# Attention of a two-layer kernel: four scores in a row, then the row maxima in groups of one and three

## The reference

```python
x = x + attn(layernorm(x))
# attn
Q = einsum('btd,hkd->bthk', x, W_Q) + b_Q        # K, V alike
scores = einsum('bqhk,bshk->bhqs', Q, K) / sqrt(64)
out_h = einsum('bhqs,bshk->bqhk', softmax(scores), V)
return einsum('bqhk,hdk->bqd', out_h, W_O) + b_O
```

## Time and profile before

| | |
|---|---|
| median of 3 runs | 1372.09 us (1371.39 to 1373.73) |
| the profiled execution's own time | 1373.44 us |
| its span, first to last instruction | 1371.1 us |
| TensorE (PE) busy | 1187.1 us, 87% |
| VectorE (DVE) busy | 919.2 us, 67% |
| ScalarE (ACT) busy | 568.5 us, 41% |
| GpSimd (POOL) busy | 749.8 us, 55% |
| exponentials, ACT L842 | 256 of 1026 ns |
| row maxima, DVE L1131 | 256 of 1225 ns |
| sums of probabilities, POOL L1572 | 180 of 2370 ns |

### The profile page before, as it was taken

How to read it: one execution, slowest core, us unless ns; L and a number is a source line. 1 busy time by engine, 2 the same in 40 slices (tenths; PEclk the granted TensorE clock), 3 DMA queues, 4 the chain that set the end, 5 groups by cost and what they waited for, 6 DMA issues and landing times. The chain is left out here.

```text
span 1371.1 us, 19083 instructions
## 1 busy us (share of the span) xinstructions
PE 1187.1 (87%) x7491; PEld 671.4 (49%) x7491; DVE 919.2 (67%) x1318; ACT 568.5 (41%) x735; POOL 749.8 (55%) x379
## 2 busy tenths in 40 slices
PE   4799979999999998999999999567876777676898
PEld 2345535555555554555555558555432333233676
DVE  4766566566566567466756445246999899996687
ACT  1244434444444445343444435238643622233544
POOL 1277756776777676465797821532754455464200
PEclk9999999999999999999999989778988889799899
DMA  5000000000000000000001142453622333240000
GB/s 173 1 1 2 1 1 1 1 1 2 1 1 2 1 1 1 2 1 1 5 9 32 55 174 76 132 215 123 203 92 92 107 110 110 93 150 0 0 17 16
DMA packets 38057, 68.82 MB, mean 50 GB/s; under 512 B 5936, under 2 KB 24112, under 8 KB 37968
## 3 DMA queue, kind: packets, MB, share of 16 engines
q1 hardware_dynamic: 32624, 47.75, 10.8%
q0 software_dynamic: 5344, 19.86, 4.1%
HBM read 61.30 MB, written 6.16 MB: 49 GB/s over the span
## 5 line engine op out<-in xcount | busy, mean ns | idle before, releaser
L1572 POOL TENSOR_TENSOR psums<-psums,prob 128x1024 f32<-128x1024 f32 x180 | 426.7, 2370 | 128.1 <-ACT prob L842 106.1
L1131 DVE TENSOR_REDUCE mx<-psum 128x2 f32<-128x1024 f32 x256 | 312.5, 1225 | 174.2 <-PE psum L458 163.7
L842 ACT ACTIVATE prob<-psum 128x1024 f32<-128x1024 f32 x256 | 261.2, 1026 | 266.3 <-PE psum L445 253.6
L472 PE MATMUL psum<-prob,V 128*64 128x512 f32 x1024 | 248.5, 605 | 0.0
L1632 POOL TENSOR_TENSOR hc<-hs,cc 128x1024 f32<-128x1024 f32 x64 | 155.4, 2427 | 167.4 <-DVE hs L1396 167.1
L700 PE MATMUL psum<-hc,ident 128*128 128x512 f32 x256 | 149.5, 714 | 53.2 <-POOL hc L1632 51.6
L1396 DVE TENSOR_TENSOR_SCAN hs<-dA,psum 128x1024 f32<-128x1024 f32 x64 | 146.3, 2286 | 2.1
L1572 POOL TENSOR_TENSOR psums<-prob 128x1024 f32<-128x1024 f32 x30 | 71.7, 2390 | 135.2 <-ACT prob L842 135.1
L441 PE MATMUL psum<-q_hi,k_hi 64*128 64x512 f32 x512 | 123.7, 473 | 1.6 <-issue 0.9
L472 PEld LDWEIGHTS psum<-prob,V 128*64 128x64 f32 x1024 | 69.1, 138 | 109.3 <-issue 105.8
L458 PE MATMUL psum<-k_hi,q_hi 64*128 64x512 f32 x512 | 109.1, 429 | 0.0
(11 more groups left out here) (234 smaller groups left out, 1693.0 us busy)
## 6 DMA issues: line engine op xcount, KB each, us to landing
cc<-C_rows SPq DMA_DIRECT2D x64, 512.0 KB, 3.7
slots_in<-e_zero SPq DMA_DIRECT2D x2, 960.0 KB, 8.6
slots_out<-e_y SPq DMA_DIRECT2D x30, 64.0 KB
slot_rows_h<-slots_in SPq DMA_DIRECT2D x6, 256.0 KB
x<-in_x SPq DMA_DIRECT2D x2, 512.0 KB, 5.2
e_w<-in_e_w SPq DMA_DIRECT2D x1, 1024.0 KB
out_x<-x SPq DMA_DIRECT2D x4, 256.0 KB, 2.3
wk<-in_wk SPq DMA_DIRECT2D x1, 512.0 KB, 4.3
```

Of the source, the lines that this page charges most:

```text
L472: ins = pe.matmul(A.O[HALF[s], :], A.V[pair % 2][:, j, s * DH:(s + 1) * DH], A.prob[unit(pair, c, j) % NPB][:, s * CH:(s + 1) * CH], start ...
L842: act.activation(A.prob[n % NPB][:, :], slots.bank("score", pair, c, j).rearrange("p s n -> p (s n)"), ACT.Exp, scale=float(DH) ** -0.5).t ...
L1131: dve.tensor_reduce(K.A.mx[:, :, t, c], slots.bank("max", pair, t, c), AXX, ALU.max).then_inc(*slots.inc("max", pair, t, c))
L1572: pool.tensor_tensor(total[:, :], (K.A.prob[(n - 1) % NPB] if j == 1 else total)[:, :], K.A.prob[n % NPB][:, :], ALU.add).then_inc(*K.psum ...
```

## The change

The order of steps within a phase is written differently. Before, the four maxima of a phase stand behind the four scores, one each, and `out` behind the last of them, ahead of the projection. Now the four scores stand in a row, one maximum behind them, then the projection and the first `pv`, then the other maxima (three; four or five in pair 0), `cols` and `out`, and then the second `pv`. `row` moves from the middle of P2 to the front of P3. `proj` is split in two steps, `proj` for TensorE and ScalarE and `lo` for VectorE, and `lo` stands right behind `proj` everywhere. P0 to P3 of pair 15 stay as they are.

```diff
@@ phase
-    order = []
-    for i, j in enumerate(js):
-        order.append(("score", pair, c, j))
-        order += [("max", *m) for m in maxes[len(maxes) * i // 4:len(maxes) * (i + 1) // 4]]
+    maxes = [("max", *m) for m in maxes]
+    order = [("row", nxt)] if f == 3 and nxt < PAIRS else []
+    order += [("score", pair, c, j) for j in js] + maxes[:1]
+    maxes = maxes[1:]
+    if pair == LAST and f == 1:
+        order += [("out", last, 0), ("out", last, 1)]
     if f == 2 and nxt < PAIRS:
-        order.append(("cols", nxt))
+        maxes.append(("cols", nxt))
     if pair < LAST and f >= 2 and last >= 0:
-        order.append(("out", last, f - 2))
-    elif pair == LAST and f == 1:
-        order += [("out", last, 0), ("out", last, 1)]
+        maxes.append(("out", last, f - 2))
     first, second, third = [], [], []
...
-        first = [("proj", ahead, *CHUNKS[(f + 1) % 4])]
+        first = [(kind, ahead, *CHUNKS[(f + 1) % 4]) for kind in ("proj", "lo")]
...
-    if f == 2 and nxt < PAIRS:
-        second = [("row", nxt)]
...
-    order += first + pv[:2] + second + pv[2:3] + third + pv[3:]
+    order += first + pv[:1] + maxes + pv[1:2] + second + pv[2:3] + third + pv[3:]
@@ plan_all
-        elif kind in ("proj", "row", "values", "sum", "sumhalf", "gdir"):
+        elif kind in ("row", "values", "sum", "sumhalf", "gdir"):
             work.plan("dve", *step)
-            if kind == "proj":
-                K.hi.plan(*k)
+        elif kind == "proj":
+            work.plan("dve", *step, now=False)
+            K.hi.plan(*k)
```

More of the change, by code:

```diff
@@ L202, in attention_order @@
     order = [("lnvar", 0), ("lnroot", 0), ("lnrows", 0), ("lnturn", 0), ("lncopy", 0), ("bias", 0)]
-    order += [("proj", 0, *ch) for ch in CHUNKS]
+    order += [(kind, 0, *ch) for ch in CHUNKS for kind in ("proj", "lo")]
     side = [("values", 0, 0), ("values", 0, 1)] + [("proj", 1, *ch) for ch in CHUNKS] + [("proj", 2, *CHUNKS[0])]
@@ L208, in attention_order @@
             order.append(side.pop(0))
+            if order[-1][0] == "proj":
+                order.append(("lo", *order[-1][1:]))
     order += [("cols", 0), ("row", 0)]
@@ L330 @@
 CHUNKED = ("fc1", "xpj", "inp", "dtp")
-EMPTIES = {"xr_out": "xr", "turned": "turn", "outp_out": "outp", "choose": "logits", "fc2_out": "fc2", "e1_lg": "e1_gate",
+EMPTIES = {"lo": "proj", "xr_out": "xr", "turned": "turn", "outp_out": "outp", "choose": "logits", "fc2_out": "fc2", "e1_lg": "e1_gate",
            "gelu": "up", "yrow": "down", "gelu1": "up1", "sum1": "sum1", "added": "turn1"}
@@ L1501, in dve_added @@
     ins.then_inc(*K.work.inc("turn1", b, c))
-DVE_STEPS = {"lnvar": dve_moments, "lnhalf": dve_half_moments, "lnrows": dve_rows, "bias": dve_bias, "proj": dve_proj, "max": dve_max, "pv": dve_late_sums, "cols": dve_cols,
+DVE_STEPS = {"lnvar": dve_moments, "lnhalf": dve_half_moments, "lnrows": dve_rows, "bias": dve_bias, "lo": dve_proj, "max": dve_max, "pv": dve_late_sums, "cols": dve_cols,
              "row": dve_row, "values": dve_values, "sum": dve_sum, "sumhalf": dve_sum_half, "out": dve_out, "gdir": dve_gdir, "choose": dve_choose,
```

## The result

| | before | after |
|---|---|---|
| median of 4 runs each, same chip | 1372.91 us (1371.39 to 1374.08) | 1390.29 us (1388.09 to 1392.08) |
| ratio | | 1.0126, 95% interval 1.0106 to 1.0147 |
| the profiled execution, and its span | 1373.44, 1371.1 | 1388.09, 1386.8 |
| ordinary pair (P0, P1, P2, P3) | 47.05 (11.82, 11.93, 12.18, 11.12) | 48.1 (11.5, 12.7, 12.1, 11.8) |

The account below looks back on a forecast made before the run. TensorE's own order of work was taken as the bound. Ordinary pairs +0.77 us, times 13 +10.0; special places +2.5 + 1.9 + 2.4 - 1.9 - 0.3 - 0.1; sum +14.5, giving 1386.6 us, range 1376 to 1397.

Parts of the forecast that it names:

- P0: First of a pair's four TensorE phases: nothing waits for VectorE, -0.38 us, to 11.44.
- P1: Second phase: the second values wait 1.1 us for VectorE, busy with the maxima; +0.72, to 12.65.
- P2 with the row: Third phase: output projection waits for VectorE's second maximum, the old row wait pays for it; -0.19, to 11.99.
- P3: Fourth phase: the same output projection wait, without the row; +0.62, from 11.12 to 11.74.
- The row: Row transpose in front of P3's scores: needs no wait, and its old wait of 0.73 us in P2 goes.
- rival 2: TensorE's clock falls behind the new waits: about 1430 us, over 1500 if three phases per pair; chance 0.05.
- Rival 1: VectorE's queue does not hold TensorE: 3.1 us less per pair than forecast, 1342 us; chance 0.06.
- Pair 0: 16 maxima in three phases, so more waits for slots and VectorE: +0.9, +1.3, +0.7, -0.4, together +2.5 us.
- Pair 10, P0: Gate transpose waits for a VectorE chain that starts at 10.0 instead of 8.0: +2.0 instead of -0.4, +2.4 us.
- Pair 2, P3: VectorE begins the second batch's norm 2.5 us later, behind maxima and output sums: +1.9 us on top of +0.6.
- The router's four waits of 0.47: First router's transposes and matmuls, pairs 9 to 11: four waits of 0.47 us go, -1.9 us.
- Pair 13: It has no projection in P3: -0.3 us against an ordinary pair.

Follow-up runs that it names:

- e3: The changed kernel with the last maximum of P1 behind the first values step (pairs 1 to 14): 1379.74 us, ratio 1.0047 to the kernel before.
- e1: The kernel before with only the row transpose moved, from P2 to in front of P3's scores: 1362.86 us, ratio 0.9927.
- e4: The changed kernel with two maxima in front of the projection and two behind the first value product: 1355.96 us, ratio 0.9881 to the kernel before.
- e5: The changed kernel with two maxima ahead of the projection in P2, P3 and pair 0, plus the edit of e3: 1322.87 us beside 1348.56, ratio 0.9814.
- e10: e2 with the eight xrows operations of pair 9 moved from P2 to the end of P1: 1366.79 us, ratio 0.9957 to the kernel before.
- e8: The changed kernel with pair 0 alone in the old order of scores and maxima: 1362.02 us, ratio 1.0104 to the kernel before.
- e2: The changed kernel with the output projection of P2 and P3 behind the second value product: 1374.83 us, ratio 1.0016 to the kernel before.
- e9: e2 with GpSimd's four additions in P3 of pair 9 on 64 columns instead of 1024: 1367.63 us, ratio 0.9975 to the kernel before.
- e6: The changed kernel with the row transpose back in P2 between the second and third value product: 1384.68 us, ratio 1.029 to the kernel before.
- e7: The changed kernel with VectorE's low half behind the second maximum in P2 and P3: 1373.69 us, ratio 1.0193 to the kernel before.

## Why the prediction was right, step by step

The direction and the size are right, and the mechanism is the one forecast, each wait at its place with its releaser.

- **P0**: 11.49, walked 11.44. Nothing waits for VectorE there.
- **P1**: 12.66, walked 12.65. The second values start 10.77 us into the phase (417.75 to 428.52), the number of the walk, and e3 shows the cause.
- **P2 with the row**: 12.11, walked 11.99; **P3**: 11.85, walked 11.74. The output projection starts at 8.03, walked 7.92: VectorE starts on the second maximum at 6.67, walked 6.64, ends at 7.90, and TensorE needs 0.13 more, not the 0.05 that I took from the values. That 0.08 and the 0.03 of VectorE, in two phases, are most of what an ordinary pair costs above the forecast: +1.05 in this one instead of +0.77 (8.0 us in the eight ordinary pairs, 1, 3 to 8 and 12, instead of 6.2).
- **The row** waits for nothing. That the old wait of 0.73 paid for the new one holds, and e1 shows it alone: 0.8 per pair.
- **The clock** stayed at 1.00 in 400 to 500 us, behind waits of up to 1.07 us, so rival 2 did not come true in the ordinary pairs. In pair 0 the clock fell in this trace (below).
- **Rival 1**, that the queue would not hold TensorE, is refuted by e3, e4 and e5: without the queue a pair takes 44.95, 3.15 less than in the kernel after. The prediction had put that at 3.1.
- **The Trainium skill** (TensorEngine Tiling (Array Packing), Key Properties) says that a change of tiling mode drains the array. The trace agrees, with a price of about 0.1: the first maximum behind a value product shows 0.49 (in e3, 419.89), the one behind scores 0.40 (421.55 above). It doesn't tell a drain from weights that could not be loaded ahead.
- **The range**: its upper end adds up to 1396.1 (1386.6 + 6.5 + 3), not 1397; nothing hangs on it.

**Terms that were mis-sized.** They lie in the special places, and offset one another in part.

Pair 0 was to cost 2.5 us and cost 4.8 (53.44 against 48.65). The walk counted waits alone. In P2 two maxima wait, for 0.95 and 0.63, and behind them TensorE's timeline and a window (length, busy us of each engine with instructions, clock, DMA share, GB/s) show:

```profile
90.91 0.51 PE L459 MATMUL psum<-k_hi,q_hi 64*128 64x512 f32 x2 [0.63 <-DVE mx L1132]
91.34 4.46 PE L473 MATMUL psum<-prob,V 128*64 128x512 f32 x12
```

```profile
90.91:95.73 4.82, 4.82 (x15) 1.32 (x15) 3.52 (x4) 0.00 (x0) 1.63 (x1) 0.65 0.01 3
```

Three value products took 4.46, 2.80 at full clock (439.54 above): the granted clock of 0.65 costs them 1.7 us, and P2 grew by 1.9 instead of 0.7. But the waits do not make the clock fall by themselves. In e10 pair 0 has the same order and the same two waits, and the clock stays at 1.00:

```profile
89.93 0.50 PE L461 MATMUL psum<-k_hi,q_hi 64*128 64x512 f32 x2 [0.63 <-DVE mx L1134]
90.36 2.79 PE L475 MATMUL psum<-prob,V 128*64 128x512 f32 x12
```

P2 of pair 0 takes 12.89 there, which is the walked length (12.22 + 0.7), and 14.09 here. P0 grew by 2.0 instead of 0.9: beside the wait of 1.05 that was walked, its scores ran at half clock until 60.49 and in the kernel before until 58.58, and 1.9 us at half clock do 0.95 less. That is not the order's doing either: in e1 and e8, with P0 of pair 0 in the old order, it takes 14.85 where the kernel before takes 13.97. P1 (+1.3) and P3 (-0.4) came as walked. So the walk of the waits held in pair 0, and nearly all of the 2.3 us that it missed is time at half clock. In e8, with pair 0 in the old order, 4.6 are back.

Pair 10, P0, was to cost 2.0 more and cost 1.1. The gate transpose waits 3.78 instead of 2.66, since the maxima stand ahead of the gate chain; but in that chain the operation that took 1.66 us in the kernel before (e_wg, 8 x 16 elements, while GpSimd was adding) takes 0.22, with GpSimd idle (its rows stand in the last section). Pair 2, P3: the norm's wait is 7.51 instead of 5.73, the phase +2.5, walked +2.5. The router's four waits of 0.47 are gone, as walked. Pair 11 came out 1.3 below its walk (52.42, before 53.41): in its P2 the kernel before spent 3.4 us at a granted clock of 0.50 (632.3 to 635.7), the kernel after none. Nothing in the walk foresaw that.

Pair 13 (+1.0) was walked as +0.5 and pair 14 (+0.6) as -0.1. The walk gives them as sums only. In pair 14 P1 grew by 0.7 (11.71 instead of 10.98), as in an ordinary pair, and P3 by 0.4 (8.74 instead of 8.37).

In sum pair 15 starts 17.9 us later (801.6 instead of 783.7) where the walk has 14.5: pair 0 +2.3 against the walk, the eight ordinary pairs +1.8, pairs 13 and 14 +1.2, pairs 9 to 11 -1.9. That misses of both signs met is luck. From there on 2.2 us are won back in the profiled execution (span +15.7); no order is changed there, other executions of the same kernel differ by as much, and what did it stays open. By the medians the change costs 17.4 us, 2.9 more than forecast.

**What stays open**: why the clock falls for longer at some of these places than at others. Kernels with the same order around pair 10 differ there: e8 takes 1.6 us more for it than the kernel after, and its P0 takes 17.96 in e2 and 19.20 in e9 and e10. Time at half clock stands behind it: a granted clock of 0.50 for 6.8 us in P0 and P1 of pair 10 in the kernel after (from 565.8), for 10.2 in e9 (from 548.0) and e10 (from 547.0). No run here shows what decides between the two, nor between the two P2 of pair 0.

## What to carry to other kernels

Ahead of a run of work for a slower engine, count how fast both engines go through it: TensorE makes a row maximum in 0.23 us, VectorE takes 1.12, and each step that needs a slot back from one of them, or stands behind them in VectorE's queue, waits for the difference. Splitting the run at the engine's idle time (two and two) cost 0.2 us in P0 (11.72 instead of 11.48), where nothing had waited, and gave 0.6 to 1.1 in each of the other phases, 2.4% in all. Give a moved step's effect per ordinary stage, but walk the irregular stages one by one, against every engine that may be in the way: here three forecasts missed by 0.6 to 1.2% for that reason (e2 and e6, whose sums per pair were right, and e7, where the sum per pair was 0.2 too high as well).

## What the runs showed of the hardware

**VectorE stands still until a GpSimd instruction ends.** The eight operations xrows (float32, SBUF to SBUF, 128 x 128) took 2.13 us with no GpSimd addition beside them, 4.32 (e5), and 6.43 (e2), steps of about 2.15: one or two of the eight stood still for an addition of about 2.4 less their own share of 0.3. With additions of 0.33 they took 2.42 (e9). It does not take a large operation: e_wg in the kernel before (8 x 16) ends at 548.48, as the second addition beside it ends (548.45), and takes 1.66 instead of 0.22.

```profile
546.82 1.66 DVE L1212 TENSOR_SCALAR e_wg<-e_wg,e_wgn 8x16 f32<-8x16 f32 x1
```

```profile
543.61 4.84 POOL L1572 TENSOR_TENSOR psums<-psums,prob 128x1024 f32<-128x1024 f32 x2
```

The reductions from PSUM beside the same additions did not change (1.21 to 1.23 each, all 256 of them in the kernel after). The Trainium skill (SBUF — State Buffer, Who interferes with whom) says that VectorE and GpSimd share a pair of ports under an exclusive lock, that a tensor_scalar can take it and that a tensor_reduce on this chip never does. The trace agrees, by the tensor_scalar rows (6.43 against 2.42) and by the reductions; how the ports are held it doesn't show. This is the rule that I should have weighed against each place where the change moves a VectorE operation past GpSimd's additions.

**The same waits, with and without a lower clock.** Waits of 0.95 and 0.63 us in P2 of pair 0 were followed by a granted clock of 0.65 over 4.8 us in the kernel after, and by 1.00 in e10. Waits of 0.95 and 0.75 in P1 of the same pair left it at 1.00, and so did one wait of 1.05 per phase in over 20 phases. A wait of 2.17 was followed by slow products in pairs 11 and 14 of e6 and not in pair 10. So the length of a wait did not tell by itself what the clock did.

**Reductions overlap**: three in 3.48 us, four in 4.61 and five in 5.74, a step of 1.12 to 1.13 where one alone takes 1.23.
